# Two chunks that meet all eight tiles in place, instead of being sorted, in a one-core attention and routed-tile kernel

## What is computed

```python
q, k, v = (gelu(h @ W1 + b1) @ W2 + b2 for each of q, k, v)      # h = layernorm(x)
scores = einsum('bid,bjd->bij', q, k) / sqrt(256 * 512) * tril
out = layernorm(einsum('bij,bjd->bid', scores, v)) * ln_w + ln_b
x = x + out
# routing: idx[s] = argmax over 8 tiles of  pe(s) . sign(tile_sigs)
y_all = einsum('bsd,tod->bsto', layernorm(x), W) + b
x = x + take(y_all, idx)                                         # tile idx[s] alone
```

## Time and profile before

| | us |
|---|---|
| median of 3 runs | 330.94 |
| lowest and highest | 329.14, 333.31 |
| the profiled execution's own time | 330.04 |
| its span, first to last instruction | 328.3 |
| TensorE busy | 289.6 (88%) |
| VectorE busy | 225.9 (69%) |
| ScalarE busy | 200.2 (61%) |
| GpSimd busy | 166.2 (51%) |

### The profile page before, as it was taken

The page is one execution under the profiler, slowest core; times in us unless marked ns, Lnnn a source line. Parts: engine busy times, 40 slices in busy tenths (PEclk is TensorE's granted clock), DMA queues, the critical chain, the costliest instruction groups (busy, mean ns, idle before and its releaser), DMA issues.

```text
span 328.3 us, 5578 instructions
## 1 busy us (share of the span) xinstructions
PE 289.6 (88%) x1828; PEld 258.7 (79%) x1828; DVE 225.9 (69%) x528; ACT 200.2 (61%) x406; POOL 166.2 (51%) x233
## 2 busy tenths in 40 slices
PE   5999999999999999999999999999988886496750
PEld 5778888997898898889798888988877865485640
DVE  3788677799789669858966885796395694244430
ACT  2487677666867785786578677687653462364300
POOL 3620803442591749366264827547437348755562
PEclk9599999999999999999999999999999799587895
DMA  8809950010012111110311001611006302671110
GB/s 213 284 3 313 334 149 0 2 64 32 24 44 66 64 35 59 37 57 10 99 59 40 0 0 35 173 40 66 34 33 195 98 32 84 198 272 63 45 55 2
DMA packets 24655, 28.00 MB, mean 85 GB/s; under 512 B 4722, under 2 KB 22386, under 8 KB 24564
## 3 DMA queue, kind: packets, MB, share of 16 engines
q1 hardware_dynamic: 15764, 13.07, 13.6%
q0 software_dynamic: 3488, 8.99, 7.8%
q10 hardware_dynamic: 5376, 5.59, 5.5%
HBM read 13.99 MB, written 14.56 MB: 87 GB/s over the span
## 4 chain that ended last, share of the span: by engine, by line
PE 66%; DVE 18%; issue 6%; ACT 3%; another core or an unknown queue 3%; DMA 2%; POOLq 0%; POOL 0%; DVEq 0%; ACTq 0%
PE ring L431 35%; PE o_ps L431 10%; PE s_ps L431 6%; PE sc_ps L431 5%; PE w_ps L431 3%; PE ring L444 2%; DMA hT<-position_table 2%; DVE xres L1092 2%; PE ring L525 2%; DVE xb L1296 1%; PE ring L652 1%; DVE st L1099 1%; DVE hT L1016 1%; PE sc_ps L652 1%
## 5 line engine op out<-in xcount | busy, mean ns | idle before, releaser
L431 PE MATMUL ring<-xnT,w_sp 128*128 128x512 f32 x288 | 74.9, 404 | 2.6 <-DVE xnT L1011 1.2
L431 PEld LDWEIGHTS ring<-xnT,w_sp 128*128 128x128 f32 x288 | 52.8, 192 | 15.8 <-issue 2.6
L769 ACT ACTIVATE ring<-ring,b_cols 128x512 f32<-128x512 f32 x48 | 31.7, 660 | 26.2 <-PE ring L431 22.3
L431 PE MATMUL ring<-hT,w_sp 128*128 128x512 f32 x192 | 46.4, 396 | 0.0
L1016 DVE TENSOR_TENSOR hT<-ring,hT 128x512 fp32r<-128x512 f32 x48 | 32.7, 684 | 16.3 <-ACT hT L772 14.7
L431 PEld LDWEIGHTS ring<-hT,w_sp 128*128 128x128 f32 x192 | 35.4, 188 | 8.1 <-DVE hT L1016 0.2
L1525 POOL DMA_INDIRECT sorted_rows<-xres,slot_i x32 | 32.7, 1021 | 9.1 <-issue 6.8
L1491 POOL TENSOR_TENSOR vtok<-v,vtok 128x512 fp32r<-128x512 f32 x14 | 17.6, 1279 | 31.0 <-ACT vtok L791 31.0
L1472 POOL TENSOR_SCALAR nm<-mv 128x4 f32<-128x4 f32 x8 | 1.8, 230 | 57.6 <-DVE mv L998 57.6
L1570 POOL DMA_INDIRECT out_dram<-slot_rows x23 | 22.7, 986 | 13.6 <-DVE slot_rows L1302 6.9
L772 ACT CAST hT<-ring 128x512 fp32r<-128x512 f32 x48 | 28.2, 587 | 1.5
(11 more groups left out here) (184 smaller groups left out, 629.0 us busy)
## 6 DMA issues: line engine op xcount, KB each, us to landing
sorted_rows<-blank ACTq DMA_DIRECT2D x1, 5070.0 KB, 19.9
xt<-x SPq DMA_DIRECT2D x8, 512.0 KB, 3.5
slot_rows<-sorted_rows SPq DMA_DIRECT2D x23, 130.0 KB
h<-sorted_rows SPq DMA_DIRECT2D x16, 130.0 KB
w_stage<-tile_w SPq DMA_DIRECT2D x8, 256.0 KB, 2.8
hT<-position_table POOLq DMA_DIRECT2D x1, 512.0 KB, 6.6
sorted_rows<-xres,slot_i POOLq DMA_INDIRECT x32
row_stage<-rows ACTq DMA_DIRECT2D x1, 384.0 KB, 8.2
```

Source lines behind the costliest of these rows:

```text
L431: last = te.matmul(o, lhs[k][a], rhs[k][c], start=start and k == 0 and i == 0, stop=stop and k == n - 1 and i == 2, skip_group_check=check)
L769: nc.scalar.activation(full, ring[(2 + m) % 3][:, :], ACT.Gelu, bias=b1c[:, m // 2, m % 2:m % 2 + 1]).then_inc(gelu, 1)
```

## The change

The last two chunks (`DENSE = 2`, the last 256 rows of the second sequence) are no longer scattered, loaded and stored by index. Their rows stay in `xres`. They are normalised, transposed and rounded in line with the blocks (as numbers 37 and 38), are multiplied by all eight tiles, two at a time in matmuls of 512 columns, and VectorE adds each tile's product times the one-hot number of that tile, 16 additions in all. SyncE stores the two chunks as plain rows. The sorted blocks are then 37, and the routing counts two chunks less in the last class. Besides, the last step's `last_out(0)`, `last_out(1)` and what follows from them move ahead in the lists of TensorE, ScalarE, VectorE and GpSimd.

```diff
+DENSE = 2
+SLOTS = NB * NJ - DENSE + NT - 1
+        def dense_rows(e):
+            return xres[LAST % XR][:, CH - DENSE + e, :]
...
@@ SyncE
+            for e in range(DENSE):
+                sp.wait_ge(dense_done, NT * (e + 1))
+                at = T - (DENSE - e) * P
+                sp.dma_start(out[NB - 1, at:at + P], dense_rows(e)[:, 0:C]).then_inc(dense_sent, 16)
+
+            sp.wait_ge(dense_sent, 16 * DENSE)
...
@@ TensorE
+            def dense_products(e, g):
+
+                n = SLOTS + e
+                i = NT // 2 * e + g
+                te.wait_ge(xb_lo, n + 1)
+                if i < 4:
+                    te.wait_ge(y_done, SLOTS + i - 3)
+                else:
+                    te.wait_ge(dense_done, 2 * (i - 3))
+                mm3(y_bank(SLOTS + i)[:, :], [[xb_all[:, n % XB, a, cols(k)] for a in range(2)] for k in range(KC)],
+                    [[wf[:, a, k, 2 * g * C:2 * g * C + 2 * C] for a in range(2)] for k in range(KC)]
+                    ).then_inc(dense_ps, 1)
...
             last_scores(1)
             last_scores(2)
-            slot_products(6)
-            slot_transposes(7)
             last_scores(3)
             last_state(0)
             last_state(1)
+            slot_products(6)
+            slot_transposes(7)
+            last_out(0)
+            last_out(1)
+            last_state(2)
             slot_products(7)
             slot_transposes(8)
-            last_state(2)
-            last_out(0)
-            last_out(1)
+            last_out(2)
+            last_state(3)
             slot_products(8)
             slot_transposes(9)
-            last_out(2)
-            last_state(3)
             last_out(3)
             slot_transposes(10)
             slot_transposes(11)
             for n in range(9, SLOTS):
-                if n + 3 < SLOTS:
+                if n + 3 < SLOTS + DENSE:
                     slot_transposes(n + 3)
                 slot_products(n)
+            for e in range(DENSE):
+                for g in range(NT // 2):
+                    dense_products(e, g)
...
@@ ScalarE
             last_rounded(2)
+            scores_rounded(LAST)
             slot_rounded(7)
-            scores_rounded(LAST)
...
@@ VectorE, route_blocks
+                link(nc.vector.tensor_tensor(held[:, :, CLASSES - 1], incl[:, :, NJ - 1 - DENSE], incl[:, :, NJ - 1],
+                                             ALU.add))
...
+            def dense_out(e, t):
+
+                i = NT // 2 * e + t // 2
+                dve.wait_ge(dense_ps, i + 1)
+                if t:
+                    dve.wait_ge(dense_done, NT * e + t)
+                j = NJ - DENSE + e
+                nc.vector.scalar_tensor_tensor(out=dense_rows(e)[:, 0:C], in0=y_bank(SLOTS + i)[:, t % 2 * C:t % 2 * C + C],
+                                               scalar=onehot[:, t, j:j + 1], in1=dense_rows(e)[:, 0:C],
+                                               op0=ALU.mult, op1=ALU.add).then_inc(dense_done, 1)
...
@@ VectorE, the last step
+            scores_rest(LAST)
             slot_out(6)
             slot_rest(7)
-            scores_rest(LAST)
+            out_centred(LAST, 0)
+            out_centred(LAST, 1)
             slot_out(7)
             slot_rest(8)
-            out_centred(LAST, 0)
-            out_centred(LAST, 1)
+            x1_final(LAST, (0, 1))
+            out_centred(LAST, 2)
+            x1_stats(LAST, (0, 1))
             slot_out(8)
-            out_centred(LAST, 2)
+            x1_var(LAST, (0, 1))
             slot_rest(9)
...
@@ GpSimd
-            slots((4, 5, 6, 7))
+            slots((4, 5, 6))
             rstd_out(LAST, (0, 1))
+            slots((7,))
+            rstd_x1(LAST, (0, 1))
+            rows_sorted(LAST, (0, 1))
             slots((8,))
             rstd_out(LAST, (2, 3))
             slots((9,))
-            rstd_x1(LAST, (0, 1))
-            rows_sorted(LAST, (0, 1))
-            slots((10, 11))
             rstd_x1(LAST, (2, 3))
-            rows_sorted(LAST, (2, 3))
-            slots(range(12, SLOTS))
+            slots(range(10, SLOTS))
```

More of the change, by code:

```diff
@@ L63 @@
 XR = 3
[L64 removed]
+SIGNED, MATCHED, SLOTTED, ROUTED = 3, 9, 34, 41
 NEAREST = float(3 << 22)
@@ L331, in mk_seq_kernel @@
         sent = [sem(f"sent{i}") for i in range(2)]
+        dense_ps = sem("dense_ps")
+        dense_done = sem("dense_done")
+        dense_sent = sem("dense_sent")
         gate_dve = sem("gate_dve")
@@ L353, in sent_before @@
         def sent_before(s):
-            return [CH * 16 * len(range(i, s, XR)) for i in range(XR)]
+            return [16 * (CH * len(range(i, s, XR)) - (DENSE if s > LAST and i == LAST % XR else 0))
+                    for i in range(XR)]
         @block.sync
@@ L979, in _ @@
             slot_norm(11)
-            for n in range(9, SLOTS):
+            for n in range(9, SLOTS + DENSE):
                 slot_rounded(n)
-                if n + 3 < SLOTS:
+                if n + 3 < SLOTS + DENSE:
                     slot_norm(n + 3)
```

23 lines of the change are left out of this document (12 added, 11 removed).

## The result

The changed kernel takes 328.96 us (median of 20 runs, 326.33 to 330.78), the kernel before 331.70 in as many runs beside it: ratio 0.9926, interval 0.9903 to 0.9949. So it is faster by 2.7 us, 0.7%: clear of the noise, and inside the band of 2% around no change. The prediction was 326.0 us, 4.9 under the median it started from, so that about half of the forecast gain came. The profiled execution has a span of 328.10 us and a time of its own of 329.80; before they were 328.30 and 330.04. The profiled execution of before was thus 1.7 us quicker than its later median and that of after 0.8 slower, so of the 2.7 us only 0.2 can be found in this pair of traces. What the pair shows well is how large terms moved inside the tail.

The account below looks back on a forecast made before the run. TensorE, busy 88% of the span, was taken to bound the body, with losses in the tail. Terms -6.9 - 2.0 - 2.8 + 11.2 - 3.0 - 0.5 = -4.0 gave span 324.3, time 326.0 us, range 319 to 332.

Parts of the forecast that it names:

- The gap: TensorE's wait for block 21's rows between products 17 and 18: 8.35 us becomes 1.41, -6.9 us.
- The same work on each engine ... -0.5: Reordered lists ahead of product 9: work unchanged, TensorE's idle for block 7 filled; -0.5 us (+0.5 to -1.5).
- what is late next is nothing that waits for memory: In the tail, with block 21 there by about 271, no later step was expected to wait for memory.
- The clock after the gap, -2.0: Products 18 to 22 took 6.85 us for 4 steps; at a faster pace -2.0 us (-3.1 to -1.2).
- the pace rival: Late results after the gap come from it, so steps to product 36 take 1.2 us: -5.5, 320.5 us; chance 0.2.
- product 36 begins at about 303: Sign for the new trace: start of the last sorted block's product; wrong if before 299 or after 307.
- The dense products: Behind product 36, 48 matmuls of 512 columns at 0.233 us each: +11.2 us (5.8 to 20.5).
- the third rival: Dense products at the lower clock: 2.56 not 1.40 us a group, +9.3 for all eight, 335.3 us; chance 0.08.
- The end, -3.0: From last product's end to span's end: 8.25 us against 11.3, with 7.2 us for SyncE's last store; -3.0 us.
- ten us before the new end: GpSimd's stores of blocks 10 to 36, 34.8 us from about 271, end at 306, off the path.
- What would have shown it wrong: Signs: product 36 begins before 299 or after 307, dense groups over 1.5 us each, or last store over 9.

Follow-up runs that it names:

- the first experiment: Changed kernel with only GpSimd's rstd_out for chunks 2 and 3 moved ahead of the scatters and block 8's store: 309.49 us, ratio 0.9738 to the kernel before.
- group 2: One chip, kernel before 332.70 us; changed kernel unedited 0.9934, with old order 0.9929, with constant tile numbers 0.9813, without GpSimd's stores behind block 9 0.9391.
- group 4: One chip, kernel before 332.44 us; changed kernel 0.9919, with GpSimd's inverse root first 0.9827, with plain stores by SyncE 0.9426, by GpSimd 0.9408.
- groups 1, 3 and 5: Edits of the changed kernel (order, stores, tile addresses) on three chips where the kernel before takes 317.3 to 318.4 us; ratios 0.9714 to 0.9978.
- The two kernels that were to tell the first: Changed kernel with blocks 10 to 36 stored indirectly to in-order places, 311.03 us, 0.9800; with every second indirect store left out, 308.30 us, 0.9714.

## Why the prediction was right or wrong

*The gap: right.* -7.1 us against -6.9. There is no wait of ScalarE for a load after 264, and product 18 starts 1.26 us after product 17. The prediction had block 21's rows at 276.8 in the old order, just when TensorE came to a stop, so that two scatters less were to do nearly all of it; with the old order and two scatters less, 17 to 18 was 2.92.

*"The same work on each engine ... -0.5": the step that failed.* Product 9 did start 0.9 us earlier, but "what is late next is nothing that waits for memory" was left there, without following the other half of the same list, and the stretch 9 to 17 was put at nothing. On GpSimd, `rows_sorted(LAST, (0, 1))` moved ahead of `rstd_out(LAST, (2, 3))`, 2.6 us of scatters in front of 1 us of small operations that VectorE, and through it TensorE, waits for. In the kernel before that order was the other way round. The cost was +5.4 us in the trace; the first experiment shows the cause (9.10 us instead of 13.95 to 14.44 in its neighbours on one chip, 10.77 instead of 17.97 on another). With the scatter's 1.3 us of the earlier trace rows and the prediction's own rule, to name what is queued behind a moved step, it could have been worked out. About 2.7 us of the 16.7 were a hold, not the wait: without stores, in group 2, the steps took 14.05. At the end of the kernel the wait is worth less than the trace says: where both ran (group 4), taking it out gave 2.3 us of the time and a kernel 5.4 us under the kernel before. The forecast was 4.9 under it and 2.7 came, so that the net price of this step is about what the forecast missed.

*The clock after the gap, -2.0: wrong.* The stretch 18 to 36 went by +0.3 us. The gap was not what made it slow. Its clock stays low (0.84) as the holds let TensorE run dry; without them (group 2, no stores) it is 1.00. VectorE and TensorE of the changed kernel:

```profile
290.78 0.42 DVE L1338 TENSOR_TENSOR slot_rows<-w_ps,slot_rows 128x256 f32<-128x256 f32 x1 [3.63 <-remote]
299.19 0.42 DVE L1338 TENSOR_TENSOR slot_rows<-o_ps,slot_rows 128x256 f32<-128x256 f32 x1 [3.42 <-PE ring L446]
...
285.71 0.96 PE L446 MATMUL w_ps<-wf,xb 128*128 x6
291.68 0.66 PE L680 MATMUL ring<-ident,xn 128*128 128x128 f32 x2 [3.15 <-DVE xb L1332]
```

The product at 285.71 is taken up at 290.78, TensorE idles 3.15 us and starts again at 291.68 at the lower clock (0.66 us for a pair of transposes). For the same reason the pace rival fell: the gap is gone, and the pace is what it was. It was right that a step of 0.94 is the natural one (0.93 wherever holds are absent), but wrong on the cause. The prediction took the holds as a property of the stretch, which was safe, and then booked 2 us as if they would not take them back. (Its mark "product 36 begins at about 303" is also 1 us off its own sum: 313.48 - 0.5 - 6.9 - 2.0 = 304.1.)

*The dense products: right in rate, +1.2 in clock.* The chain of waits of the changed kernel at the end:

```profile
311.27 1.03 PE ring L446 x6
312.29 2.56 PE w_ps L446 x6
314.85 1.47 PE o_ps L446 x6
316.32 1.40 PE s_ps L446 x6
...
323.32 1.42 PE ring L446 x6
324.74 0.02 issue
324.76 0.49 DVE xres L1347
```

Six groups stand at 1.40 to 1.42 us, 0.233 a matmul, as the earlier trace rows had it; neither figure of the Trainium skill ("TensorE: Matmul & The Clock Gate", "Back-to-back issue gap", 216 ns isolated and 131 ns sustained for 512 columns) is met, the first nearly. The first group is at the lower clock and takes 2.56, the very price that the third rival named; a hold (2.18 us up to 309.13) and 1.74 us of idle TensorE up to 310.04 stand ahead of it, and it stayed at one group. That the hold did it is likely and not shown: in group 2 the same kernel has a hold of 3.07 us up to 310.73 and no slow group. 12.45 us instead of 11.2. The rest of the +10.1 is that product 36 and its hand-over took 1.2 us and not 0.7. VectorE's pair took 1.07 us a group, near the 1.02 reckoned.

*The end, -3.0: mis-sized by 4.9.* The 7.2 us from the last store's start to the span's end were taken for SyncE's too. The trace of before held the answer in the rows that the prediction did not read: SyncE's drain at 323.5 against GpSimd's to 328.1. A plain store by SyncE costs 2.2 us to the end, the drain of GpSimd 5.6 to 6.0 behind its last DMA. GpSimd's row of stores was put off the path for a reason that doesn't hold: from 271 at 1.29 us each it would end at 306, "ten us before the new end", but the prediction's own end is 324.3, and the ten us are to its last matmul. In the trace the row ended at 316.43, held up by the late results, and was still hidden; on the chips without holds, where the wait was taken out, this row and its drain end the kernel. The gift at the end and the -0.9 at the head nearly paid for the new wait, the missing clock term and the slow group: against the prediction -4.9 - 0.4 - 0.2 on one side and +5.4 + 2.3 + 1.7 on the other make +3.9, which leaves -0.2 of the -4.0 (to rounding).

So the sign and the range (319 to 332) held, by errors that cancel, which is luck; of the sum only the first term and the rate of the dense matmuls were right. What would have shown it wrong did: product 36 began at 311.11, after 307, and the mean dense group took 1.56 us.

*Better than both.* With GpSimd's inverse root ahead of the scatters the kernel is at 0.9827 on a chip with holds and at 0.9725 to 0.9738 on chips without: faster than the kernel before on both kinds, and 2.3 us faster than the changed kernel where the two ran side by side.

*What stays open.* Which part of an indirect store makes the hold (reading the index table, the scattered rows, the dropped blank rows, or how closely they follow each other), and why the chips of groups 1, 3 and 5 do not show it. The two kernels that were to tell the first ran only where there are no holds. How much of the 7.1 us of the gap each part of the change has is only bounded by one trace. That the holds feed back what is won ahead of 18 is seen in two kernels (the old order, and the inverse root first), without a mechanism. Whether `slot_out(9)` put back ahead of `x1_final(LAST, (2, 3))` on VectorE would have been enough against the new wait was not tried.

## What to carry to other kernels

When a step is moved in one engine's list, follow every small operation that it now stands in front of: a 1 us operation that another engine waits for goes ahead of a DMA issue of 1.3 us. Try the last DMA of a kernel on SyncE (here 2.1 us less than on GpSimd, by the nearest pair of runs), and read at each engine's closing drain which one ends the span. And before a wait is priced, ask whether what it frees is lost again downstream, where another limit (here held results) sets the time.

## What the runs showed of the hardware

- GpSimd's closing drain ends 5.6 to 6.0 us behind its last DMA instruction in most traces (before 5.96, changed 5.64), also with plain stores (5.80), and 4.5 to 4.8 us in four (no stores, half of the stores twice, plain stores by SyncE in group 4). In three traces in which GpSimd had the last DMA it ended 4.3 to 4.7 us after SyncE had seen everything land.
- On some chips, with GpSimd's indirect stores beside them, VectorE takes up a matmul's result 1 to 4 us late every few products: 18 steps take 29 to 33 us and not 16.7. With as many plain stores of 128 KB by GpSimd or SyncE it doesn't happen. The kernel before runs in 331.7 to 332.7 us on such chips and in 317.3 to 318.4 on the others, 4.5% apart.
- After 4.18 us of idleness TensorE's granted clock was at its lower level (0.53 from 270.3 to 273.7), and product 11 took 1.55 us instead of 0.96 to 0.98. After 3.15 us (at 291.68) it was too (0.52 to 294.5). Each time it came back within a few products.
